# Output projection of an attention block moved into the attention's loop over token tiles, with silu rebuilt from tanh

## The reference

```python
        attn = jax.nn.softmax(scores - (1.0 - soft_mask) * MASK_PENALTY, axis=-1)
        out = sum((attn[..., w][..., None] * v_pad[:, w:w + L].reshape(B, L, H, D) for w in range(K)))
        out = out.reshape(B, L, C)
        return silu(out @ Wout)
    ...
    x = _layernorm(x + _L0_attn_ref(x, ...), axis=-1)
    x = _layernorm(x + _L0_ffn_ref(x, ...), axis=-1)
```

## Time and profile before

| what | value |
|---|---|
| two timed runs | 2302.60 and 2422.46 us, median 2362.53 us |
| the profiled execution | 2304.26 us, its span 2302.7 us (slowest core) |
| spans of the 8 cores | 2281.7 to 2302.7 us |
| TensorE busy | 1535.8 us, 67% of the span |
| VectorE busy | 542.2 us, 24% |
| ScalarE busy | 563.7 us, 24% |
| GpSimd busy | 117.5 us, 5% |
| output projection, first half | first matmul at 550.98 us, last square's row sum read from 583.82 us |

### The profile page before, as it was taken

One profiled execution on the slowest core, in us unless ns is written; L12 is line 12 of the kernel. 1 busy time (PEld: TensorE's weight loads), 2 busy tenths in 40 slices (PEclk: granted clock), 3 DMA queues, 4 the chain that ended last, 5 costly groups with the idle time before them and its releaser, 6 DMA issues.

```text
span 2302.7 us, 22758 instructions; the slowest of 8 cores (2281.7 to 2302.7 us)
## 1 busy us (share of the span) xinstructions
PE 1535.8 (67%) x8376; PEld 788.6 (34%) x8492; DVE 542.2 (24%) x814; ACT 563.7 (24%) x836; POOL 117.5 (5%) x136
## 2 busy tenths in 40 slices
PE   0595254448466989889807923445474879889895
PEld 0242133224433434344304412323234434344442
DVE  0164212101311221222212442211022121222223
ACT  0353122224321112121204521222242202121122
POOL 0120000000200000000001100000001000000000
PEclk9997555556578999999957955555575989999997
DMA  9222211230182525530292222121204525534203
GB/s 219 55 38 37 76 41 48 57 56 1 20 127 37 74 38 80 85 54 1 38 230 31 37 60 59 36 68 36 55 1 70 77 40 78 78 62 74 37 1 109
DMA packets 142341, 139.37 MB, mean 61 GB/s; under 512 B 73239, under 2 KB 106136, under 8 KB 142234
## 3 DMA queue, kind: packets, MB, share of 16 engines
q0 software_dynamic: 60960, 84.55, 23.6%
q1 hardware_dynamic: 76890, 36.60, 6.4%
q10 hardware_dynamic: 4384, 16.78, 2.2%
HBM read 189.36 MB, written 33.10 MB: 97 GB/s over the span
## 4 chain that ended last, share of the span: by engine, by line
PE 61%; DMA 18%; DVE 7%; ACT 6%; issue 5%; another core or an unknown queue 2%; SPq 1%; DVEq 0%; ACTq 0%; POOL 0%; POOLq 0%
PE ps_A L336 37%; PE ps_B L336 14%; PE ps_t L342 9%; DVE bscr L364 3%; DMA scdram<-swide 3%; DMA wpool<-Su 3%; ACT R L355 2%; DMA R<-awdram 2%; DMA qpark<-Wd 2%; DMA wpool<-Wd 2%; DMA wrf<-Wr 1%; DMA wpool<-Sd 1%; DMA bscr<-x 1%; DVE xtm L364 1%
## 5 line engine op out<-in xcount | busy, mean ns | idle before, releaser
L336 PE MATMUL ps_A<-wpool,R 128*128 128x512 bf16 x2118 | 498.9, 386 | 36.9 <-DMA wpool<-Su 18.2
L355 ACT COPY R<-ps_t 128x512 bf16<-128x512 bf16 (+2 forms) x242 | 186.4, 784 | 787.1 <-PE ps_t L342 730.3
L342 PE MATMUL ps_t<-sb_ident,bscr 128*128 128x128 bf16 x1312 | 147.0, 264 | 335.7 <-DVE bscr L364 208.7
L336 PEld LDWEIGHTS ps_A<-wpool,R 128*128 128x128 bf16 x2176 | 211.2, 99 | 281.4 <-issue 54.9
L336 PE MATMUL ps_B<-wpool,R 128*128 128x512 bf16 (+1 forms) x1072 | 239.7, 369 | 42.1 <-DMA wpool<-Sd 26.6
L351 ACT ACTIVATE fscr<-ps_A 128x512 f32<-128x512 f32 x236 | 140.7, 599 | 437.4 <-PE ps_A L336 425.8
L342 PEld LDWEIGHTS ps_t<-sb_ident,bscr 128*128 128x128 bf16 x1312 | 112.8, 118 | 388.6 <-issue 356.1
L336 PE MATMUL ps_A<-qpark,R 128*128 128x512 bf16 x750 | 179.0, 382 | 3.9 <-DVE xtm L364 2.9
L336 PEld LDWEIGHTS ps_B<-wpool,R 128*128 128x128 bf16 x1088 | 101.6, 100 | 168.0 <-issue 59.9
L342 PE MATMUL ps_t<-sb_ident,R 128*128 128x128 bf16 (+1 forms) x384 | 74.5, 289 | 85.4 <-DMA R<-awdram 80.8
L336 PE MATMUL ps_A<-R 128*128 128x64 bf16 (+1 forms) x512 | 86.7, 228 | 57.8 <-ACT R L355 57.8
(11 more groups left out here) (133 smaller groups left out, 1291.0 us busy)
## 6 DMA issues: line engine op xcount, KB each, us to landing
scdram<-swide SPq DMA_DIRECT2D x16, 648.0 KB, 2.9
xtm<-x ACTq DMA_DIRECT2D x2, 4096.0 KB, 29.3
wpool<-Wkv POOLq DMA_DIRECT2D x4, 2048.0 KB, 34.8
qpark<-Wg POOLq DMA_DIRECT2D x8, 1024.0 KB, 29.2
kpark<-Wu POOLq DMA_DIRECT2D x8, 1024.0 KB, 34.1
wpool<-Wg POOLq DMA_DIRECT2D x8, 1024.0 KB, 15.8
wpool<-Wu POOLq DMA_DIRECT2D x8, 1024.0 KB, 20.9
qpark<-Wd POOLq DMA_DIRECT2D x8, 1024.0 KB, 9.6
```

Of the source, the lines that this page charges most:

```text
L336: e.matmul(d, l, r, start=s0, stop=s1),
L342: P.op("tensor", lambda e, d=dst, s=src: e.transpose(d, s, ident[:]), rd=[src, ident[:]], wr=[dst], tag=tag, strips=strips)
L355: P.op("scalar", lambda e, o=out, i=in_: e.copy(o, i), rd=[in_], wr=[out], tag=tag)
```

## The change

The separate stage for the output projection goes. A function `emit_W(i)` does one tile of it, and is called from the attention loop: in turn i, for i from 3 on, `emit_W(i - 3)` stands between `emit_B(i - 2)` and `emit_A(i)`. Tiles 0 to 4 are thus done in the loop; tile 5 comes between the last two calls of `emit_B`, tiles 6 and 7 come after them.

Each tile uses one PSUM bank for both of its groups of matmuls (the third bank of `ps_A` for even tiles, of `ps_B` for odd ones), so that the second group waits until the first one has been read. Silu is no longer one ScalarE instruction: a tanh on ScalarE, then on VectorE a multiply-add and a product with the matmul's result in PSUM. The table loaded ahead of the loop holds exp and tanh in place of ln and exp, and the table load for silu goes.

```diff
-            table(AF.Ln, AF.Exp)
+            table(AF.Exp, AF.Tanh)
...
+            wob = [ps_A[:, 1024:1536], ps_B[:, 1024:1536]]
+
+            def emit_W(i):
+                ao_fm = qpark[:, 1024 * i:1024 * (i + 1)]
+                pg = wob[i % 2]
+                th = fscr[i % 2]
+                for gi in range(2):
+                    for c in range(8):
+                        mm(pg, ao_fm[:, 128 * c:128 * c + 128],
+                           WOUT[:, 1024 * c + 512 * gi:1024 * c + 512 * gi + 512],
+                           c == 0, c == 7, tag=f"wo{hx}")
+                    act(th[:, 512 * gi:512 * gi + 512], pg, AF.Tanh, scale=0.5,
+                        tag=f"woth{hx}")
+                    vop("tensor_scalar", th[:, 512 * gi:512 * gi + 512],
+                        [th[:, 512 * gi:512 * gi + 512], 0.5, 0.5],
+                        (ALU.mult, ALU.add), tag=f"wosg{hx}")
+                    vop("tensor_tensor", th[:, 512 * gi:512 * gi + 512],
+                        [th[:, 512 * gi:512 * gi + 512], pg], (ALU.mult,),
+                        tag=f"wosl{hx}")
+                xsl = xtm[:, 1024 * i:1024 * (i + 1)]
+                vop("scalar_tensor_tensor", xsl, [th[:], 1.0, xsl],
+                    (ALU.bypass, ALU.add), accum=u1st[:, i:i + 1], tag=f"u1{hx}")
+                act(qfm[0][:], xsl, AF.Square, accum=u1st[:, NT + i:NT + i + 1],
+                    tag=f"u1sq{hx}")
...
                 if i >= 2:
                     emit_B(i - 2)
+                if i >= 3:
+                    emit_W(i - 3)
                 emit_A(i)
             emit_B(NT - 2)
+            emit_W(NT - 3)
             emit_B(NT - 1)
-
-            ck(6)
-            table(AF.Silu)
...
+            emit_W(NT - 2)
+            emit_W(NT - 1)
```

## The result

The changed kernel is slower. Its time is 2431.65 us (median of 11 runs), against 2307.03 us for the kernel before (10 runs, measured beside it); the ratio is 1.053, 95% interval 1.050 to 1.056, so 5.3% or 123 us. The forecast was 2412 us and slower. Some executions of each kernel ran some per cent slower on one half of the cores or on both; the ratios leave them out, while the medians count them (without them the two medians are 2427.65 and 2305.40 us).

The account below looks back on a forecast made before the run. The prediction took a ring of waits in the attention loop, with no engine full, as the bound. Five turns at 11.5 us plus 7.6 minus 11.0 gave 54.1 us per half, 2412 us from 2304.3; range 2380 to 2455.

Parts of the forecast that it names:

- The ring: Attention loop: exp, norm, k and q transposes, scores, score writes, weight read, emit_B, exp; anything inserted lengthens each turn fully.
- The chain from E: emit_W in a loop turn: exp starts at E + 12.5 instead of E + 1.0, so a turn grows by 11.5 us.
- E: The end of the last transposes of emit_B in a turn, from which the added work is timed.
- Which clock: emit_W's matmuls: clock rises at the first group's end, second group at upper clock; without a rise, 12.9 us a turn.
- every group cold: Rival: all emit_W matmul groups at the lower clock, 12.9 us a turn, 64 us per half, 2432 us; chance 0.25.
- The sum: Whole kernel: 57.5 + 7.6 - 11.0 = 54.1 us per half, 108 for two, giving 2412 us, 4.7% more.
- Tiles 5 to 7: End of each half: tile 5 between the last emit_B calls costs 7.6 us; tiles 6 and 7 save 11.0 us.
- The table load: Removed silu load ahead of the separate stage: covered by the wait for the first matmul group, counted as zero.
- Hidden in idle time: Rival: projection fits TensorE's 14 us idle a turn, turns cost nothing, 2282 us; chance 0.04.
- the clock stays up: Rival: upper clock holds across the loop, saving at most 9 us a turn, 2322 us; chance 0.04.

Follow-up runs that it names:

- the stage with the rebuild alone: Kernel before, its separate stage kept, with tanh, multiply-add and product in place of silu and no silu table load: 2342.2 us, ratio 1.012.

## Why the prediction was right, point by point

- **The ring, and that nothing in it is hidden: shown.** The step said that whatever is put between two members is paid in full. In the changed kernel the weight wait stayed at 8.72 us; three places for the same instructions cost 12.3, 8.2 and 1.5 us a turn; the experiment with one matmul of eight shows that even TensorE's work was paid while TensorE was idle half of the time.
- **The chain from E: right to 0.2 us where the clock did as assumed.** Predicted at E: first tanh 3.5, second 7.5, exp 12.5. Measured in turn 3 of the profiled core: 3.5, 7.6, 12.4. The multiply-add, which was bounded by 0.29 and 0.90 and taken as 0.49, took 0.43.
- **Which clock: the step that was mis-sized.** I took the rise at the end of the first group and the second group at the upper clock. Among the 80 turns with an `emit_W` on the eight cores that is what 13 did: the clock rose in the gap between the groups, and the second group ran wholly at the upper clock (under 2.1 us from its first matmul to its tanh). In 50 turns it rose within the first group or just at its end, and fell again inside the second. In 17 it did not rise at all for a tile, and the second group took over 3.6 us. The mean over the 80 was 2.94 us where I had 1.9 to 2.0. The second tanh came 5.01 us behind the first and not 4.0; the first tanh came 3.29 us behind E, 0.2 earlier than I had it, and from the second tanh to the exp it took 4.8 us where I had 5.0. So the exp stood 13.1 us behind E on average and not 12.5, and a turn grew by 12.3 us and not 11.5. I had taken the 4.7 us of the fall behind the separate stage for the time that it always has. With two banks, where the gap is gone, neither happened in any of the 80 turns, so both come with the 2.16 us in which TensorE waits for VectorE. Turns 5 and 6 of the profiled core show one of each (columns as in the earlier trace rows; in turn 5 the groups start at 447.90 and 452.71, in turn 6 at 500.37 and 505.72):

```profile
449.00:450.00 1.00, 1.00 (x4) 0.34 (x3) 0.00 (x0) 0.00 (x0) 0.00 (x0) 0.57 0.00 0
...
452.00:453.00 1.00, 0.29 (x2) 0.20 (x3) 0.56 (x1) 0.00 (x0) 0.00 (x0) 1.00 0.00 0
453.00:454.00 1.00, 1.00 (x5) 0.41 (x4) 0.00 (x0) 0.00 (x0) 0.00 (x0) 0.64 0.00 0
454.00:455.00 1.00, 1.00 (x4) 0.29 (x2) 0.00 (x0) 0.00 (x0) 0.00 (x0) 0.50 0.00 0
...
501.00:503.00 2.00, 2.00 (x7) 0.59 (x4) 0.00 (x0) 0.25 (x1) 0.00 (x0) 0.50 0.00 0
503.00:505.00 2.00, 0.56 (x2) 0.00 (x0) 0.54 (x2) 0.60 (x1) 0.00 (x0) 0.50 0.00 0
507.00:509.00 2.00, 2.00 (x6) 0.69 (x5) 0.00 (x0) 0.00 (x0) 0.00 (x0) 0.50 0.00 0
```

  In turn 5 the clock is up at the end of the first group, through the gap, and down in the middle of the second; in turn 6 it stays at 0.50 throughout. My rival "every group cold", with 0.25, was thus true of 17 turns in 80, and the mean of the second group lies nearer to its value than to my forecast's. The Trainium skill, page "TensorE: Matmul & The Clock Gate", section "Loop structure matters more than you think", has matmuls run cold when long waits part them: the trace agrees in these 17 turns, while in the other 63 the clock rose.
- **The sum and the slowest core.** The mean of the cores grew by 118 us, between the 108 of my forecast and the 128 of that rival: 8 of the 10 us between 108 and 118 are the ten turns at 0.8 us each, and the ends, at 1.3 us a half, are about the rest. No step of the prediction dealt with the core that is slowest. In the two profiled executions it stood 9 and 20 us above the mean, but ten executions of the changed kernel have 9 to 27 us (median 13) and twelve of the kernel before 6 to 22 (median 10), so part of these 11 us is chance. That the measured 2432 us is the rival's figure to the microsecond is luck too: it is made of a mean that grew by 10 us less than the rival's sum, and of a slowest core that neither sum has. It is inside the stated range and 4 us beyond the range that I gave for the forecast alone.
- **Tiles 5 to 7.** The end was to be 3.4 us shorter per half (11.0 less 7.6); it was 2.1. From one set of last transposes to the next, tile 5 cost 8.2 us and not 7.6; tiles 6 and 7 took 23.0 us from the last transposes to the last square and not 22.2. The second groups of tiles 5 and 6 took 3.07 us on average where I had 1.9 to 2.0, the same clock term; what set it off in part was not followed up.
- **The table load** was priced at nothing, and the stage with the rebuild alone, which also lost its load, grew by 15.6 us behind the last transposes, all of it the vector work (8 tiles, 5.5 us each and not 3.55 from square to square).
- **The rivals.** "Hidden in idle time" and "the clock stays up" fell: the k transposes moved from 5.6 to 16.9 us behind E, where less than 3 us was the mark, and the long stretches of a turn stay at 0.50.

## What to carry to other kernels

Where no engine is full, find the ring of waits first and put new work only where the engine that must do it, and every engine behind it in the chain, is waiting for something else. In this kernel the wait for the score writes and the read of the weights was such a place, the wait for another engine of the same ring was not. An idle share says nothing on this; the same instructions cost 12.3, 8.2, 1.5 or 0 us by their place. When two groups of matmuls must follow each other, give them two banks: here the gap cost its own length, 2.1 us, and half as much again through the clock.

## What the runs showed of the hardware that was not expected

- The granted TensorE clock held through a gap of 2.16 us and then fell while matmuls ran again (453 to 454 us above) in 50 of 80 turns, and did not rise at all in 17. With a gap of 0.84 us it rose and stayed up to the end of the second group in 68 of 80, with no gap in all 80.
- Cores that do the same work meet the clock at different moments: in the same turn (turn 3 of the first half) the second group took 2.0 us on the profiled core, 2.7 on core 0 and 3.7 on core 5. Whether this is what sets the slowest core apart was not tried. The spans of the eight cores lie 20 to 42 us apart in ten executions of the changed kernel (median 31) and 14 to 56 in twelve of the kernel before (median 20).
